# Order of half-height and full-height matrix products in an expert part and a latent stage, and identity products at another wait

## The chip, the cores and the metric

The kernel runs on one core of a Trainium2 chip. The metric is device time in microseconds (us) of one launch, median of several runs; lower is better. A profiled execution supplies the trace.

## The reference, cut to what matters

A small language-model tower on 32 tiles of 128 token rows, 192 features: embedding, an attention, a local-expert attention, then the three parts below.

```python
# latent stage (L), ends with a gated feed-forward network
latent = silu(x_norm @ w_comp);  qkv = latent @ w_qkv            # decayed linear attention ...
x = x + attn_out
xn = rmsnorm(x, ffn_ln_w)
x = x + (silu(xn @ w1) * (xn @ w2)) @ w3                         # 192 -> 512 -> 192
# expert attention (M): 12 heads of 16, softmax, router of 8 experts, top 2
logits = xm @ router_w.T + router_b
# expert part (X)
for e in range(E):
    h = gelu(xm @ w1[e] + b1[e]);  y = h @ w2[e] + b2[e]         # 192 -> 768 -> 192
    out = out + combine[:, e:e + 1] * y
```

## The kernel before

All arithmetic is in float32 in these parts, and each float32 product stands in the trace as two TensorE records (two passes), a transpose as one. Every engine has a program written out by hand; semaphores order them, and `per(g, n, k)` is the value to wait for in turn g.

**Two streams (L and M).** The 32 tiles make 16 pairs. Two streams of pairs, `streams[0]` and `streams[1]`, each own four PSUM banks (`a.bank[0..3]`), and `first(...)` of one pair is interleaved with `second(...)` of the other: the programs are Python generators, `alternate` runs them in turns up to each `yield`, and this fixes the order on every engine. `in_turns_apart(eng, first, second, over, ...)` (L) and `in_turns_routed` (M) are the outer loops: a peeled start, a hardware loop of 7 turns (6 in M) with two pairs each, a peeled end. `over()` is called after the peeled start, at the end of each turn and at the very end.

**Latent stage, hidden layer.** `hidden(a, f, p)` (L1660 to L1669) is called for p = 0 and 1. The 192 input features lie as 128 (`xT[:, 0]`) and 64, the latter doubled into both halves of the partitions (`xT[:, 1]`). For each of `lw_1` and `lw_2` it issues two full-height products (L1665, 128 rows of contraction) and then two half-height ones (L1668, 64 rows, in the two halves of the array, into two banks). ScalarE's silu of it is L1796, VectorE's product L1615. Just behind `hidden` in TensorE's order stand the transposes L1691 of the other pair, which wait for VectorE's L1558. ScalarE's program of the stage uses Identity (L977), Silu (L1743, L1796) and Exp (L1765), and table loads stand in it where the function table changes.

**Expert attention.** `scores(... turned=True)` (L1987) makes the scores of tile 0 and then of tile 1 of the pair; ScalarE exponentiates them (L2116, four per tile). The scores of tile 1 wait for the four exponentials of tile 0, since they use the same banks; between the two stand the router products of the other pair (L2075). `m_times_v` (L2000) of tile 0 waits for the first exponential of tile 1. `stirred(a, n)` (L2015) issues n products of the identity matrix with itself whose result nobody reads; they fill waits. Two stand before the wait for `f.x` (normalised rows, VectorE L1856) at the head of `tensor_m_1`, which the transposes L966 follow.

**Expert part.** The rows that the router sent to each expert are taken in 39 groups of 256 rows, three buffers deep (`h` = 0 to 2), 13 turns of three. For each group SyncE loads the expert's weights (L2267) and rows (L2271) as soon as the group three before it is out (`x_out`); VectorE doubles 64 columns of the rows (L2226); TensorE turns them (L2300, L2301, bank 6); ScalarE takes them out (L2359). TensorE's group is: `up` p = 0 and 1, the turning of the next group's rows, `down` 0, `up` 2, `down` 1, `down` 2. One `up` is two full-height products (L2316) and two half-height ones (L2320), 256 columns each, into banks 0 and 1 (p = 0, 2) or 2 and 3; ScalarE's gelu is L2368. One `down` is four products of 192 columns (L2331) into banks 4 and 5. VectorE weights the result (L2220) and GpSimd adds it to DRAM rows by two indirect transfers (L2249); before the next group's it waits until both have landed (`x_add`).

Of the kernel before, what the change touches and what calls it, by code (L numbers as in the profile page):

```python
# [16 lines left out]
P = 128  # L17
T = 32
D = 192
# [76 lines left out]
def tower(nc, a, out):  # L96

    with ExitStack() as ctx:
# [1245 lines left out]
        def scalar_rest(act):  # L1344
            act.wait_ge(s_loop, 1)
            act.wait_ge(s_wf, 16 * len(loads_f))
            in_turns_apart(act, lambda g, a: scalar_f_1(act, g, a, f_signals(a)),
                           lambda g, a: scalar_f_2(act, g, a, f_signals(a)), at_end=lambda: scalar_l_rates(act))
            scalar_ends(act, F_ENDS, F_SEMS, L_STARTS)
            scalar_l_powers(act)  # L1350
            in_turns_apart(act, lambda g, a: scalar_l_1(act, g, a, l_signals(a)),
                           lambda g, a: scalar_l_2(act, g, a, l_signals(a)))
            act.wait_ge(s_wm, 16 * len(loads_m))
            scalar_ends(act, L_ENDS, L_SEMS, M_STARTS)
            in_turns_routed(act, lambda g, a, prev: scalar_m_1(act, g, a, m_signals(a), prev),
                            lambda g, a, prev: scalar_m_2(act, g, a, m_signals(a), prev),
                            lambda g, a: scalar_routed(act, g, a, m_signals(a)))
            scalar_x(act)
# [301 lines left out]
        def hidden(a, f, p):  # L1660

            for wa, wb, out in ((lw_1a, lw_1b, slice(0, NM)), (lw_2a, lw_2b, slice(NM, 2 * NM))):
                for n in range(2):
                    c = 2 * p + n
                    nc.tensor.matmul(a.bank[c][:, out], wa[:, c * P:(c + 1) * P], a.xT[:, 0, :], start=True, stop=False)  # L1665
                for n in range(2):
                    s = slice(HE * n, HE * (n + 1))
                    mm = nc.tensor.matmul(a.bank[2 * p + n][:, out], wb[s, p * P:(p + 1) * P], a.xT[s, 1, :], start=False,  # L1668
                                          stop=True)  # L1669
            mm.then_inc(f.hid_p, 1)  # L1670
# [34 lines left out]
        def tensor_l_2(pe, g, a, f):  # L1705
# [16 lines left out]
            mm.then_inc(f.ffn_p, 1)  # L1722

# [293 lines left out]
        def tensor_m_1(pe, g, a, f, prev):  # L2017
            stirred(a, 2)
# [30 lines left out]
            yield  # L2049
            pe.wait_ge(f.exp, per(g, 4 * M, 4))  # L2050
            scores(pe, g, a, f, 1, f.scoresT, True)
            stirred(streams[1 - a.n], 2)
# [125 lines left out]
        def vector_x(v, ch):  # L2178
# [28 lines left out]
            def outputs(g, h, first=False):  # L2207
# [11 lines left out]
                for t in range(NT):  # L2219
                    ins = nc.vector.scalar_tensor_tensor(out=x_y[h][:, t, :], in0=bank[4 + t][:, 0:D], scalar=w(t),  # L2220
                                                         in1=x_y[h][:, t, :], op0=ALU.mult, op1=ALU.add)
# [70 lines left out]

        def tensor_x(pe):
# [11 lines left out]
            def up(g, h, p, first=False):  # L2305
                if p == 0:
                    pe.wait_ge(x_xT, per(g, B3, h + 1))
                    pe.wait_ge(x_w[h], per(g, 96, 96))
                    if h > 0 or not first:
                        pe.wait_ge(x_gelu, per(g, B3 * PAIRS, h * PAIRS))  # L2310
                elif p == 2:
                    pe.wait_ge(x_gelu, per(g, B3 * PAIRS, h * PAIRS + 1))
                b = (0, 2, 0)[p]
                for n in range(2):
                    q = p + PAIRS * n
                    nc.tensor.matmul(bank[b + n][:, 0:NR], xw_1a[h][:, q * P:(q + 1) * P], x_T[h][:, 0, :], start=True,  # L2316
                                     stop=False)
                for n in range(2):
                    s = slice(HE * n, HE * (n + 1))
                    mm = nc.tensor.matmul(bank[b + n][:, 0:NR], xw_1b[h][s, p * P:(p + 1) * P], x_T[h][s, 1, :], start=False,  # L2320
                                          stop=True)
                mm.then_inc(x_up, 1)

            def down(g, h, p):
# [3 lines left out]
                for n in range(2):  # L2328
                    f = p + PAIRS * n
                    for t in range(NT):  # L2330
                        mm = nc.tensor.matmul(bank[4 + t][:, 0:D], x_hid[f][:, t * P:(t + 1) * P], xw_2[h][:, f, :],  # L2331
                                              start=(p == 0 and n == 0), stop=(p == PAIRS - 1 and n == 1))
# [3 lines left out]
            def group_of(g, h, more, first=False):  # L2336
                up(g, h, 0, first)
                up(g, h, 1)
                if more:
                    turn_rows(*((g, h + 1) if h < B3 - 1 else (g + 1, 0)))  # L2340
                down(g, h, 0)
                up(g, h, 2)
                down(g, h, 1)
                down(g, h, 2)
# [10 lines left out]
        def scalar_x(act):  # L2355
# [7 lines left out]
            def group_of(g, h, more):  # L2363
                for p in range(PAIRS):
                    act.wait_ge(x_up, per(g, B3 * PAIRS, h * PAIRS + p + 1))
                    for n in range(2):
                        q = p + PAIRS * n
                        ins = nc.scalar.activation(x_hid[q], bank[(0, 2, 0)[p] + n][:, 0:NR], ACT.Gelu,  # L2368
                                                   bias=xb_1[h][:, q:q + 1])
                    ins.then_inc(x_gelu, 1)  # L2370
                    if p == 1 and more:
                        take_rows(*((g, h + 1) if h < B3 - 1 else (g + 1, 0)))
# [142 lines left out]
```

## Time and profile before

| | |
|---|---|
| median of 3 runs | 2048.46 us (2047.97 to 2050.29) |
| profiled execution | 2050.18 us |
| its span in the trace | 2048.5 us |
| mean granted TensorE clock | 0.862 of full speed |
| TensorE busy, matmul | 1606.7 us (78%) |
| VectorE busy | 1309.3 us (64%) |
| ScalarE busy | 976.1 us (48%) |
| GpSimd busy | 400.1 us (20%) |
| latent stage | about 705 to 1200 us of the span |
| expert attention | about 1215 to 1630 us |
| expert part | about 1655 to 2048 us |

The profiled execution took 1.7 us more than the median. A granted clock of 1.00 is 2.4 GHz, 0.50 is 1.2 GHz; a mean between them is a mix of stretches at either level.

### The profile page before, as it was taken

The page shows a single profiled execution, that of the slowest core. Times are in us where ns is not written, and L with a number is a line of the kernel's source. Part 1 is how long each engine was busy: PE and PEld are TensorE (multiplying, and loading weights), DVE is VectorE, ACT ScalarE, POOL GpSimd, SP SyncE. Part 2 cuts the span into 40 slices and gives each one's busy share as a digit, 9 for nine tenths or more (in the row PEclk, how much of TensorE's full clock was granted, in tenths as well). Part 3 has the DMA queues.
Part 4 walks back from the last instruction along what each step waited for, and adds up shares of the span by engine and source line. Part 5 has one row for each costly group of instructions (what it writes and reads, how often), then busy time and mean ns, then how long its engine had stood idle before and what let it go on. Part 6 is the DMA issues. An engine that isn't in the chain of part 4 may idle for free.

```text
span 2048.5 us, 36437 instructions
## 1 busy us (share of the span) xinstructions
PE 1606.7 (78%) x12540; PEld 1167.9 (57%) x12540; DVE 1309.3 (64%) x4361; ACT 976.1 (48%) x2773; POOL 400.1 (20%) x494
## 2 busy tenths in 40 slices
PE   0166673978888668888888868999999769999996
PEld 0032222865665445555555547777877647777774
DVE  7898885878888777887787844666666622222121
ACT  1275998944444444455555423344444324444441
POOL 7302332000000100000000010222222223333332
PEclk9985555557788779999999978999999979999998
DMA  3000001049960000000000000000000057777775
GB/s 73 16 1 1 1 1 17 6 95 185 181 97 0 1 1 1 0 0 0 0 0 0 0 26 1 25 24 23 23 23 27 20 138 178 179 181 175 185 175 128
DMA packets 136262, 113.00 MB, mean 55 GB/s; under 512 B 29416, under 2 KB 128456, under 8 KB 136136
## 3 DMA queue, kind: packets, MB, share of 16 engines
q1 hardware_dynamic: 119320, 91.70, 19.4%
q0 software_dynamic: 16864, 20.33, 5.2%
q8 instruction: 41, 0.67, 0.1%
q14 instruction: 37, 0.30, 0.1%
HBM read 69.19 MB, written 45.94 MB: 56 GB/s over the span
## 4 chain that ended last, share of the span: by engine, by line
PE 51%; DVE 27%; ACT 15%; issue 4%; POOL 1%; DMA 0%; DVEq 0%; ACTq 0%; POOLq 0%; SPq 0%
ACT bank L716 8%; PE bank L2331 8%; PE bank L1007 6%; PE bank L2316 5%; PE bank L2320 4%; PE bank L1987 3%; PE bank L1000 2%; PE bank L1217 2%; PE bank L1665 2%; PE bank L966 2%; DVE R L1839 2%; DVE WK L1581 1%; DVE R L1581 1%; PE bank L2015 1%; PE bank L2000 1%
## 5 line engine op out<-in xcount | busy, mean ns | idle before, releaser
L1047 POOL TENSOR_TENSOR WK<-WK,mhalf 128x2 f32<-128x2 f32 (+1 forms) x96 | 78.0, 813 | 837.4 <-DVE WK L1505 328.3
L2368 ACT ACTIVATE R<-bank,R 128x256 f32<-128x256 f32 x234 | 98.3, 472 | 217.9 <-PE bank L2320 217.9
L2220 DVE SCALAR_TENSOR_TENSOR WK<-bank,R,WK 128x192 f32<-128x192 f32 x78 | 28.9, 412 | 266.6 <-PE bank L2331 266.6
L716 ACT ACTIVATE bank<-bank,nbias,sc 128x128 f32<-128x128 f32 x384 | 168.9, 952 | 21.7 <-POOL nbias L528 21.7
L1007 PE MATMUL bank<-WK,R 96*128 96x256 f32 x576 | 159.1, 421 | 17.0 <-ACT WK L973 11.0
L2249 POOL DMA_INDIRECT moe_sum<-WK x78 | 121.6, 1558 | 258.4 <-DVE WK L2220 197.2
L2331 PE MATMUL bank<-R 128*128 128x192 f32 x936 | 169.1, 331 | 0.0
L716 ACT ACTIVATION_READ_ACCUMULATOR bank<-bank,nbias,sc 128x1 f32 x384 | 162.2, 727 | 0.0
L2331 PEld LDWEIGHTS bank<-R 128*128 128x128 f32 x936 | 150.1, 190 | 13.3 <-issue 13.3
L1007 PEld LDWEIGHTS bank<-WK,R 96*128 96x128 f32 x576 | 111.3, 204 | 41.6 <-ACT WK L973 15.6
L2316 PE MATMUL bank<-R 128*128 128x256 f32 x468 | 126.1, 392 | 1.1 <-ACT R L2359 1.1
L610 PE MATMUL bank<-R 32*128 32x128 bf16 x384 | 62.8, 300 | 60.1 <-ACT bank L716 57.2
L610 PEld LDWEIGHTS bank<-R 32*128 32x128 bf16 x384 | 29.5, 118 | 118.8 <-ACT bank L716 106.7
L2316 PEld LDWEIGHTS bank<-R 128*128 128x128 f32 x468 | 84.5, 192 | 21.1 <-issue 13.2
L1665 PE MATMUL bank<-WK,R 128*128 128x256 f32 x256 | 75.8, 420 | 15.0 <-ACT WK L993 15.0
L433 DVE TENSOR_REDUCE neg_all<-bank 128x3 f32<-128x384 f32 x128 | 69.4, 553 | 27.4 <-PE bank L610 25.2
L966 PE MATMUL bank<-ident,WK 128*96 128x128 f32 x320 | 55.0, 299 | 40.5 <-DVE WK L1030 26.1
L2320 PE MATMUL bank<-R 64*128 64x256 f32 x468 | 83.2, 433 | 0.0
L1987 PE MATMUL bank<-WK 32*128 32x128 f32 x1536 | 64.0, 297 | 24.4 <-ACT R L2116 12.3
L559 PE MATMUL bank<-R,wq 96*128 96x512 bf16 x192 | 78.6, 537 | 4.6 <-DVE WK L407 2.7
L1000 PE MATMUL bank<-R,WK 96*128 96x192 f32 x384 | 76.3, 343 | 2.9 <-ACT WK L973 1.4
L528 POOL TENSOR_SCALAR nbias<-neg_all,sc 128x3 f32<-128x3 f32 x128 | 38.8, 303 | 198.3 <-DVE neg_all L433 198.0
(496 smaller groups left out, 3971.2 us busy)
## 6 DMA issues: line engine op xcount, KB each, us to landing
moe_rows_in<-zeros SPq DMA_DIRECT2D x1, 25026.0 KB, 146.2
R<-in_L_ffn_w SPq DMA_DIRECT2D x39, 576.0 KB, 5.0
R<-in_L_ffn_w SPq DMA_DIRECT2D x39, 384.0 KB, 3.0
R<-moe_rows_in SPq DMA_DIRECT2D x39, 194.0 KB, 4.7
R<-in_L_ffn_w SPq DMA_DIRECT2D x78, 96.0 KB, 3.7
R<-in_L_ffn_b SPq DMA_DIRECT2D x39, 96.0 KB, 5.4
moe_sum<-resid POOLq DMA_DIRECT2D x16, 192.0 KB
moe_sum<-WK POOLq DMA_INDIRECT x78, 5.9
```

The costliest lines, as they stand in the source:

```text
L610: mm = nc.tensor.matmul(bank[u % 4][:, k * P:(k + 1) * P], qk[32 * j:32 * j + 32, k, i * P:(i + 1) * P], qk[32 * j:32 * j + 32, 3 + k, i * ...
L716: ins = nc.scalar.activation(s, s, ACT.Exp, bias=nbias[:, u, k:k + 1], scale=col(SS), accum_out=units(sum_all, g, u)[:, k:k + 1])
L966: mm = nc.tensor.transpose(a.bank[b][0:C, c * NM + i * P:c * NM + (i + 1) * P], src[:, i, c * C:(c + 1) * C], ident[:, :])
L1000: mm = nc.tensor.matmul(a.bank[b][:, i * D:(i + 1) * D], a.xT[0:C, c, i * P:(i + 1) * P], w[0:C, c, :], start=(c == 0), stop=(c == 1))
L1007: mm = nc.tensor.matmul(out, w[0:C, c, m], a.xT[0:C, c, :], start=(c == 0), stop=(c == 1))
L1665: nc.tensor.matmul(a.bank[c][:, out], wa[:, c * P:(c + 1) * P], a.xT[:, 0, :], start=True, stop=False)
L1987: mm = nc.tensor.matmul(a.bank[j][:, k * P:(k + 1) * P], x, y, start=True, stop=True)
L2249: pool.indirect_dma_start(out=acc, out_offset=bass.IndirectOffsetOnAxis(ap=x_id[k % B3][:, t:t + 1].bitcast(U32), axis=0), in_=x_y[k % B3] ...
L2316: nc.tensor.matmul(bank[b + n][:, 0:NR], xw_1a[h][:, q * P:(q + 1) * P], x_T[h][:, 0, :], start=True, stop=False)
L2320: mm = nc.tensor.matmul(bank[b + n][:, 0:NR], xw_1b[h][s, p * P:(p + 1) * P], x_T[h][s, 1, :], start=False, stop=True)
L2331: mm = nc.tensor.matmul(bank[4 + t][:, 0:D], x_hid[f][:, t * P:(t + 1) * P], xw_2[h][:, f, :], start=(p == 0 and n == 0), stop=(p == PAIRS ...
L2368: ins = nc.scalar.activation(x_hid[q], bank[(0, 2, 0)[p] + n][:, 0:NR], ACT.Gelu, bias=xb_1[h][:, q:q + 1])
```

## The change

1. Latent stage: `hidden` issues, for p = 0, all four full-height products and then all four half-height ones; for p = 1 the half-height ones first and then the full-height ones.
2. Latent stage, ScalarE: `over` is now one Silu of 128x1, at the end of the peeled start and of each turn.
3. Expert attention: the two identity products at the head of `tensor_m_1` and the two before the first product with values go; five are put before the wait for the exponentials of tile 0.
4. Expert part: a group is now all six half-height products (`up_rests`, banks 0 to 5), then `up` 0, 1, 2 (full height only), the turning of the next rows, and `down` 0, 1, 2, which go to one bank (7). All gelus of the group before must be done before `up_rests`. ScalarE takes the turned rows after its third gelu pair, not after the second.

```diff
                           lambda g, a: scalar_l_1(act, g, a, l_signals(a)),
-                           lambda g, a: scalar_l_2(act, g, a, l_signals(a)))
+                           lambda g, a: scalar_l_2(act, g, a, l_signals(a)), lambda: scalar_l_silu())
...
+        def scalar_l_silu():
+            nc.scalar.activation(still[:, 1:2], mhalf[:, 0:1], ACT.Silu)
...
         def hidden(a, f, p):
+            first, second = slice(0, NM), slice(NM, 2 * NM)
+            def wholes():
+                for w, out in ((lw_1a, first), (lw_2a, second)):
+                    for c in (2 * p, 2 * p + 1):
+                        mm = nc.tensor.matmul(a.bank[c][:, out], w[:, c * P:(c + 1) * P], a.xT[:, 0, :], ...)
+                return mm
+            def rests():
+                for w, out in ((lw_1b, first), (lw_2b, second)):
+                    for n in range(2):
+                        s = slice(HE * n, HE * (n + 1))
+                        mm = nc.tensor.matmul(a.bank[2 * p + n][:, out], w[s, p * P:(p + 1) * P], a.xT[s, 1, :], ...)
+                return mm
+            if p == 0:
+                wholes()
+                rests().then_inc(f.hid_p, 1)
+            else:
+                rests()
+                wholes().then_inc(f.hid_p, 1)
...
         def tensor_m_1(pe, g, a, f, prev):
-            stirred(a, 2)
             pe.wait_ge(f.x, per(g, 1, 1))
...
             scores(pe, g, a, f, 0, f.scoresT, True)
             yield
+            stirred(streams[1 - a.n], 5)
             pe.wait_ge(f.exp, per(g, 4 * M, 4))
             scores(pe, g, a, f, 1, f.scoresT, True)
-            stirred(streams[1 - a.n], 2)
             pe.wait_ge(f.exp, per(g, 4 * M, 5))
             m_times_v(a, f, 0)
...
+            def up_rests(g, h, first=False):
+                pe.wait_ge(x_xT, per(g, B3, h + 1))
+                pe.wait_ge(x_w[h], per(g, 96, 96))
+                if h > 0 or not first:
+                    pe.wait_ge(x_gelu, per(g, B3 * PAIRS, h * PAIRS))
+                for p in range(PAIRS):
+                    for n in range(2):
+                        s = slice(HE * n, HE * (n + 1))
+                        nc.tensor.matmul(hidden_at(p, n), xw_1b[h][s, p * P:(p + 1) * P], x_T[h][s, 1, :], ...)
+            def up(h, p):
+                for n in range(2):
+                    q = p + PAIRS * n
+                    mm = nc.tensor.matmul(hidden_at(p, n), xw_1a[h][:, q * P:(q + 1) * P], x_T[h][:, 0, :], ...)
                 mm.then_inc(x_up, 1)
...
-                        mm = nc.tensor.matmul(bank[4 + t][:, 0:D], x_hid[f][:, t * P:(t + 1) * P], xw_2[h][:, f, :],
+                        mm = nc.tensor.matmul(bank[7][:, t * D:(t + 1) * D], x_hid[f][:, t * P:(t + 1) * P], xw_2[h][:, f, :],
...
             def group_of(g, h, more, first=False):
-                up(g, h, 0, first)
-                up(g, h, 1)
+                up_rests(g, h, first)
+                for p in range(PAIRS):
+                    up(h, p)
                 if more:
                     turn_rows(*((g, h + 1) if h < B3 - 1 else (g + 1, 0)))
-                down(g, h, 0)
-                up(g, h, 2)
-                down(g, h, 1)
-                down(g, h, 2)
+                for p in range(PAIRS):
+                    down(g, h, p)
...
-                    if p == 1 and more:
-                        take_rows(*((g, h + 1) if h < B3 - 1 else (g + 1, 0)))
+                if more:
+                    take_rows(*((g, h + 1) if h < B3 - 1 else (g + 1, 0)))
```

## Rows read from the trace of the kernel before

**Rows 1.** Timeline of TensorE's matmuls over one group: start, us, line, operation, count.

```profile
1800.30 1.03 PE L2316 MATMUL bank<-R 128*128 128x256 f32 x4
...
1804.60 1.03 PE L2316 MATMUL bank<-R 128*128 128x256 f32 x4
1805.55 0.70 PE L2320 MATMUL bank<-R 64*128 64x256 f32 x4
1806.19 1.13 PE L2316 MATMUL bank<-R 128*128 128x256 f32 x4
1807.25 0.70 PE L2320 MATMUL bank<-R 64*128 64x256 f32 x4
...
1808.37 1.47 PE L2331 MATMUL bank<-R 128*128 128x192 f32 x8
1809.68 1.03 PE L2316 MATMUL bank<-R 128*128 128x256 f32 x4
```

**Rows 2.** Groups of instructions, 1700 to 1950 us: half-height weight loads.

```profile
L2320 PEld LDWEIGHTS bank<-R 64*128 64x128 f32 x320 | 24.1, 184 | 26.5 <-issue 26.5
```

**Rows 3.** Timeline of the other engines, same group and the next.

```profile
1804.80 0.74 DVE L2220 SCALAR_TENSOR_TENSOR WK<-bank,R,WK 128x192 f32<-128x192 f32 x2 [7.47 <-PE bank L2331]
...
1806.30 0.84 ACT L2368 ACTIVATE R<-bank,R 128x256 f32<-128x256 f32 x2 [2.15 <-PE bank L2320]
...
1808.16 1.55 POOL L2249 DMA_INDIRECT moe_sum<-WK  x1 [0.30 <-issue]
...
1815.43 0.23 DVE L2226 COPY R<-R 128x128 f32<-128x128 f32 x1 [0.52 <-DMA R<-moe_rows_in]
...
1815.68 1.55 POOL L2249 DMA_INDIRECT moe_sum<-WK  x1 [5.96 <-DVE WK L2220]
```

**Rows 4.** DMA issues, 1700 to 1950 us: count, median us to landing.

```profile
moe_sum<-WK POOLq DMA_INDIRECT x54, 5.9
```

**Rows 5.** DMA issues, 2012 to 2036 us, where no loads run beside them.

```profile
moe_sum<-WK POOLq DMA_INDIRECT x6, 3.5
```

**Rows 6.** Groups of ScalarE, 720 to 1200 us: two of its table loads.

```profile
L977 ACT ACT_TABLE_LOAD x7 | 9.0, 1283 | 0.1
L1743 ACT ACT_TABLE_LOAD x7 | 9.0, 1283 | 0.1
```

**Rows 7.** Timeline around such loads.

```profile
931.02 1.13 PE L1007 MATMUL bank<-WK,R 96*128 96x256 f32 x4 [0.57 <-ACT WK L977]
932.28 0.38 ACT L1743 ACTIVATE R<-bank 128x256 f32<-128x256 f32 x1
```

**Rows 8.** Timeline behind the hidden layer of the latent stage.

```profile
914.41 1.03 DVE L1558 SCALAR_TENSOR_TENSOR WK<-WK 128x384 f32<-128x384 f32 x2
...
915.17 1.53 PE L1691 MATMUL bank<-ident,WK 128*128 128x128 f32 x12
...
917.44 0.95 PE L1639 MATMUL bank<-R 32*128 32x128 f32 x24 [0.74 <-ACT R L1769]
...
918.53 1.01 DVE L1581 TENSOR_TENSOR WK<-bank,decay 128x384 f32<-128x384 f32 x2
```

**Rows 9.** Timeline of TensorE in the expert attention (PEld is the weight load).

```profile
1473.90 0.95 PE L1987 MATMUL bank<-WK 32*128 32x128 f32 x24 [0.71 <-ACT R L2116]
...
1475.46 0.86 PE L2000 MATMUL bank<-R 128*32 128x128 f32 x24
...
1476.93 0.39 PEld L966 LDWEIGHTS bank<-ident,WK 128*96 128x96 f32 x4 [0.15 <-DVE WK L1856]
```

**Rows 10.** Busy time by stretch: stretch, length, PE, PEld, DVE, ACT, POOL, granted clock, DMA.

```profile
1255.14:1601.71 346.57, 321.73 (x3498) 273.51 (x3497) 227.09 (x891) 142.24 (x337) 88.05 (x106) 0.96 0.07 23
1448.69:1452.10 3.41, 3.31 (x40) 2.83 (x44) 1.49 (x9) 1.63 (x5) 1.01 (x1) 0.50 0.00 0
1356.11:1404.54 48.43, 44.53 (x503) 37.83 (x501) 33.00 (x131) 20.22 (x49) 13.26 (x16) 1.00 0.07 25
1404.54:1454.83 50.29, 47.09 (x502) 40.21 (x501) 33.00 (x131) 20.43 (x49) 13.26 (x16) 0.93 0.07 24
```

More of the change, by code:

```diff
@@ L1660, in hidden @@
         def hidden(a, f, p):
[L1662 to L1670, printed above, removed]
+            first, second = slice(0, NM), slice(NM, 2 * NM)
+            def wholes():
+                for w, out in ((lw_1a, first), (lw_2a, second)):
+                    for c in (2 * p, 2 * p + 1):
+                        mm = nc.tensor.matmul(a.bank[c][:, out], w[:, c * P:(c + 1) * P], a.xT[:, 0, :], start=(p == 0 and w is lw_1a),
+                                              stop=(p == 1), skip_group_check=True)
+                return mm
[3 more added lines that the diff above has]
+                        s = slice(HE * n, HE * (n + 1))
+                        mm = nc.tensor.matmul(a.bank[2 * p + n][:, out], w[s, p * P:(p + 1) * P], a.xT[s, 1, :],
+                                              start=(p == 1 and w is lw_1b), stop=(p == 0), skip_group_check=True)
+                return mm
[5 more added lines that the diff above has]
+                wholes().then_inc(f.hid_p, 1)
         def tensor_l_1(pe, g, a, f):
@@ L2219, in outputs @@
                 for t in range(NT):
-                    ins = nc.vector.scalar_tensor_tensor(out=x_y[h][:, t, :], in0=bank[4 + t][:, 0:D], scalar=w(t),
+                    ins = nc.vector.scalar_tensor_tensor(out=x_y[h][:, t, :], in0=bank[7][:, t * D:(t + 1) * D], scalar=w(t),
                                                          in1=x_y[h][:, t, :], op0=ALU.mult, op1=ALU.add)
@@ L2291, in sync_x, with hidden_at @@
             sp.wait_ge(x_end_st, 16)
+        def hidden_at(p, n):
+            return bank[2 * p + n][:, 0:NR]
         def tensor_x(pe):
@@ L2303, in turn_rows @@
                 mm.then_inc(x_turned, 1)
[L2305 to L2313, printed above, removed]
+            def up_rests(g, h, first=False):
[6 more added lines that the diff above has]
+                        s = slice(HE * n, HE * (n + 1))
+                        nc.tensor.matmul(hidden_at(p, n), xw_1b[h][s, p * P:(p + 1) * P], x_T[h][s, 1, :], start=True, stop=False)
+            def up(h, p):
                 for n in range(2):
                     q = p + PAIRS * n
[L2316 to L2321, printed above, removed]
+                    mm = nc.tensor.matmul(hidden_at(p, n), xw_1a[h][:, q * P:(q + 1) * P], x_T[h][:, 0, :], start=False, stop=True)
                 mm.then_inc(x_up, 1)
@@ L2330, in down @@
                     for t in range(NT):
-                        mm = nc.tensor.matmul(bank[4 + t][:, 0:D], x_hid[f][:, t * P:(t + 1) * P], xw_2[h][:, f, :],
-                                              start=(p == 0 and n == 0), stop=(p == PAIRS - 1 and n == 1))
+                        mm = nc.tensor.matmul(bank[7][:, t * D:(t + 1) * D], x_hid[f][:, t * P:(t + 1) * P], xw_2[h][:, f, :],
+                                              start=(p == 0 and n == 0 and t == 0), stop=(p == PAIRS - 1 and n == 1),
+                                              skip_group_check=True)
                 if p == PAIRS - 1:
@@ L2367, in group_of @@
                         q = p + PAIRS * n
-                        ins = nc.scalar.activation(x_hid[q], bank[(0, 2, 0)[p] + n][:, 0:NR], ACT.Gelu,
-                                                   bias=xb_1[h][:, q:q + 1])
+                        ins = nc.scalar.activation(x_hid[q], hidden_at(p, n), ACT.Gelu, bias=xb_1[h][:, q:q + 1])
                     ins.then_inc(x_gelu, 1)
-                    if p == 1 and more:
-                        take_rows(*((g, h + 1) if h < B3 - 1 else (g + 1, 0)))
+                if more:
+                    take_rows(*((g, h + 1) if h < B3 - 1 else (g + 1, 0)))
             take_rows(0, 0)
```

## The prediction

> **What bounds the kernel now.** I read the page's clock and busy rows first, then the chain of waits stage by stage, then timelines. Three stages are touched, and each has another limit.
>
> In the expert part TensorE sets the pace. The group that has its second `up` at 1800.30 is followed by the same step at 1809.68: a period of 9.38 us [rows 1], and there are 39 groups. No matmul of these rows carries a wait of its own; its time is products plus something at each change between full and half height. The other engines wait for it: VectorE 7.47 us, ScalarE 2.15 us, GpSimd 5.96 us [rows 3].
>
> In the latent stage the chain of waits goes back and forth between ScalarE, VectorE and TensorE, so only what lies on it counts. On it, once per turn, stand ScalarE's table loads before L977 and L1743 [rows 6, 7].
>
> In the expert attention the clock drops. Two turns of two pairs each, the same work: 48.43 us at clock 1.00, 50.29 us at a mean of 0.93 [rows 10]. One 3.41 us stretch at half clock (the 1.2 GHz level) begins at 1448.69, behind router products that stream 8 columns and a wait for exponentials such as the idle 0.71 us [rows 9]. The reader is to see that this wait costs little by itself, and that a half-clock stretch follows it.
>
> **Expert part, step by step.** From the starts [rows 1]: four full-height records that come from full-height work last 0.95 until the half-height ones; four that come from half-height work last 1.06; so entering costs 0.11. Four half-height records, two at a time, last 0.64 including an entry and an exit: 1.06 less 0.64 is two full passes, 0.21 each, and 0.95 less four of them leaves about 0.1 for the exit. Eight records of 192 columns take 1.31, or 0.164 each, which is 0.218 for 256 columns: the same pass, 0.215. A change of height thus costs 0.20 in all. Before, a group changes height six times (three `up`s, in and out). After, twice. Nothing else is added on TensorE: 18 pass times (12 full, 6 pairs of halves) at 0.215, 24 at 0.164, four turns at 0.11 and two changes give 3.87 + 3.94 + 0.43 + 0.40 = 8.64; the same sum with six changes gives 9.44 against the measured 9.38. Saving: 4 x 0.20 = 0.80 a group, 39 x 0.80 = 31 us. New period 8.58.
>
> What must stay hidden. Count from the start of the half-height run: it ends at 1.5, the `up`s end at about 2.4, 3.2 and 4.1, the turning at 4.6, the `down`s at 5.9, 7.2, 8.6. Two gelus take 0.84 [rows 3], so they end at about 3.5, 4.4 and 5.2; `down` needs them at 4.6, 5.9 and 7.2. The smallest slack is 1.1 us. The new wait of `up_rests` for all gelus needs 5.2 against 8.6. Row take-out ends near 6.3, needed at 8.6; a table load of about 1.3 behind it is covered as well. One output bank in place of two: VectorE is done 0.9 us into the next group, `down` writes at 4.6. The next rows: output done at 1805.54, doubled copy at 1815.43 to 1815.66 [rows 3], 10.1 us later. TensorE turns them now 11.7 us after the output (its period of 9.38, plus 3.3 to the turning, less 0.9) and after the change 8.6 + 4.2 - 0.8 = 12.0. Turning later in the group pays for the shorter period. That is why I price the transfers at nothing; if they grew by 2 us, the excess would be paid in every group.
>
> The tight one is GpSimd. It issues its second indirect transfer at 1808.16, 0.30 + 1.55 after the first (so 1806.31), waits for it to land, and needs about 0.7 to restart (the first came 0.77 after the output was done, 1804.80 + 0.74): with the median landing of 5.9 [rows 4] a cycle of 8.5; the period before is an upper bound, since at 1815.68 VectorE released it, not the transfer [rows 3]. So its cycle is 8.5 to 9.3, against 8.58 needed. But without loads beside it a landing takes 3.5 [rows 5], so a late transfer meets the idle tail of each load burst and gets faster, and it has three buffers to be late in. I take no loss; the bound is 0.4 us a group.
>
> The price of a long half-height run isn't in the trace, which has only runs of two pairs. Nearest rows: a pass pair of 0.215 (two loads of 0.184 overlap) up to 0.32, if each pair paid the entry. The four loads are recorded 184 ns each [rows 2] while the whole block of four lasts 0.64, so they overlap. I take 0.215.
>
> The Trainium skill speaks against this: "TensorE: Matmul & The Clock Gate", Part 3, says that a weight load overlaps matmuls in flight only where the row group differs, so that in a long run of half-height products, every second load would have to wait for its own half. No row of before settles it for half height.
>
> **Latent stage.** Hidden layer: eight changes of height per pair become two (one in the middle, since p = 0 ends and p = 1 begins with halves, one back, and the transposes follow full-height work), so the block is 6 x 0.20 = 1.2 us shorter. But the transposes L1691 behind it start at 915.17, and they need the first half of L1558 (914.41 + 0.52 = 914.93): only 0.24 can be won. Further on, VectorE's L1581 could start at the end of L1639, 918.39, and starts at 918.53 [rows 8], so of it 0.14 to 0.24 comes through. 15 pairs x 0.15 = 2.3, and the last pair, alone, gets its whole 1.2.
>
> Silu: the table state at the loop's head is now the same from both sides, so I expect the seven loads at L977 and the seven at L1743 to go [rows 6]. The added Silu of one column, under the 0.38 of L1743's 256, lies where TensorE is still busy with L1000. TensorE was idle 0.57 before L1007 for L977 and L1743 started 0.13 after L1007's end (931.02 + 1.13); without loads both go, and the matmuls' modelled tail (1.13 less an entry and four passes, 0.16) overlaps: 0.70 to 0.86 a turn [rows 7]. Seven turns x 0.86 = 6. Together 9 us, bounds 5 and 12.
>
> **Expert attention.** Five identity products are ten records of 128 columns, half a pass each: 1.08 us, and about 0.2 to change to the scores' shape. They fill the 0.71 of waiting and 0.16 of the tail before it, so the scores of tile 1 (L1987, 1473.90) come 0.4 later. Behind them the exponentials and L2000 shift alike, from 1475.46 to 1475.86; the two products that stood there are gone. L2000 then ends near 1476.7, and L966 waits for VectorE's L1856 until 1476.93 in any case [rows 9]. The delay ends there, with 0.2 us to spare; without that cover it would cost 16 x 0.4 = 6 us. The removed products at the head won nothing either, for the same reason. What counts is the clock: between 1255.14 and 1601.71 lie 14 pairs in 346.57 us, mean clock 0.96 [rows 10]. A turn of two pairs without a half-clock stretch takes 48.43, so seven take 339.0. So half-clock stretches cost 7.5 us here. Five products in the poorest place should remove nearly all: 7 us, bounds +6 (they stay and the delay surfaces) and -9 (one more at the stage's start goes too).
>
> **Sum.** 31 + 9 + 7 = 47 us off the profiled 2050.2 gives 2003; the median lies 1.7 lower than that execution: 2001.5.
>
> **The rivals.**
> GpSimd's transfers become the bound of the expert part: a cycle of 9.0 saves 0.38 a group, 15 us in place of 31: 2017. For it: the 8.5 to 9.3 above. Against: the lateness heals itself.
> The smaller edits do nothing: table loads stay (they are placed by the program's builder, not by the kernel's text) and the clock drops stay: 2001.5 + 6 + 7 = 2014.5. Against: the expert attention's loop has none, though Exp is used there.
> Each half-height pair pays 0.32: 6 x 0.105 = 0.63 of the 0.80 is eaten, 0.17 x 39 = 7 us are left, the hidden layer's 3.5 are lost: 2029.
> Slower: weight loads and passes of one half don't overlap. A pair then takes load and matmul, 0.184 + 0.215 = 0.40, up to 0.43 with what a change drains. At 0.43 the six pairs add 1.29 and save 0.80: +0.49 x 39 = 19; the hidden layer +4; tables and clock -13: 2050.2 + 10 - 1.7 = 2058. It decides from 0.35 in the expert part alone, and from about 0.41 over the kernel. For it: the cited rule. Against: full-height loads overlap the pass before, and the first pair in a run is issued together.
>
> **How the numbers follow.** Forecast 0.69, GpSimd 0.12, small edits 0.10, half-height 0.32 0.05, slower 0.04. The likeliest spans 1993 (33, 13, 9 saved) to 2011. The range adds GpSimd's and the small edits' cases: 1993 to 2019, leaving out about 0.12. Within 0.2% is 4 us, about what a measurement of this kernel can tell from no change. Faster 0.94; same 0.02, where the pair takes about 0.40; slower 0.04.
>
> **What would show it.** The period of L2316 blocks 8.6; one run of twelve L2320 records in about 1.5 us; GpSimd released by its own transfer in many groups, with a landing near 6. No table loads at L977 and L1743 in the loop; L1691 released by L1558. L966 still released by L1856, mean clock near 1.00 in the attention's loop. Wrong would be: a run of halves of over 2 us; ScalarE or a row transfer as releaser of TensorE in the expert part; clock drops in new places.

## The result and the profile after

The changed kernel takes 2002.2 us (median of four runs, 2001.13 to 2004.31); the kernel before took 2048.45 beside it (2047.97 to 2050.29). The ratio is 0.9774 [0.9757, 0.9791]: 46 us less. The forecast was 2001.5, its range 1993 to 2019.

The profiled execution has a span of 2000.0 us, against 2048.5 before. Cut at ScalarE's first latent row, at the attention's first exponential, at the first doubled copy of rows and at the last output, the 48.5 us of difference in span lie as follows:

| stretch | before | after | difference | forecast |
|---|---|---|---|---|
| up to the first latent row of the latent stage (no line of it changed) | 720.4 | 718.3 | -2.1 | 0 |
| latent stage | 525.5 | 520.0 | -5.6 | -9 |
| expert attention | 412.6 | 401.9 | -10.7 | -7 |
| expert part, to its last output | 371.6 | 341.8 | -29.8 | -31 |
| what follows | 18.4 | 18.1 | -0.3 | 0 |

The sum was right to a microsecond; the terms were not. Two errors cancelled: the latent stage took 3.4 us more than forecast, the attention 3.7 less.

**Expert part.** TensorE's timeline of one group (start, busy time, line, shapes, count, in brackets the idle time before it and what ended it). It answers to [rows 1]; L2334 are the half-height products, L2339 the full-height ones, L2349 `down`:

```profile
1796.38 4.07 PE L2349 MATMUL bank<-R 128*128 128x192 f32 x24
1800.38 1.57 PE L2334 MATMUL bank<-R 64*128 64x256 f32 x12
1801.87 2.86 PE L2339 MATMUL bank<-R 128*128 128x256 f32 x12
1804.57 0.27 PE L2321 MATMUL bank<-ident,R 128*128 128x128 f32 x1
...
1805.00 4.07 PE L2349 MATMUL bank<-R 128*128 128x192 f32 x24
1809.00 1.57 PE L2334 MATMUL bank<-R 64*128 64x256 f32 x12
```

From 1800.38 to 1809.00 is a period of 8.62 us; the forecast was 8.58. Twelve half-height records last 1.49 from their start to that of the next block. The runs of four in [rows 1] last 0.64, two passes and 0.21 of changing; with the same 0.2 in it, the run of twelve has 1.29 for six pairs, 0.215 each: two halves still share one pass.

GpSimd's waits between 1700 and 1950 us (waiting engine and line, released by; us in total, times, longest), first after:

```profile
POOL moe_sum L2266 <- DMA moe_sum<-WK: 140.1, 27, 6.1
POOL moe_sum L2266 <- DVE WK L2237: 15.6, 3, 5.2
```

then the kernel before:

```profile
POOL moe_sum L2249 <- DVE WK L2220: 124.2, 21, 6.1
POOL moe_sum L2249 <- DMA moe_sum<-WK: 29.8, 5, 6.0
```

The releaser has changed sides, as forecast: in 27 of 30 waits it is now GpSimd's own transfer. TensorE doesn't notice: between 1700 and 1950 us it has no wait in the trace, before or after.

**Latent stage.** The table loads between 720 and 1200 us (count; us in total and mean ns; idle before):

```profile
L1783 ACT ACT_TABLE_LOAD x16 | 20.5, 1283 | 0.3
L1814 ACT ACT_TABLE_LOAD x15 | 19.2, 1283 | 0.3
L1740 ACT ACT_TABLE_LOAD x1 | 1.3, 1283 | 0.0
```

The fourteen of [rows 6] are gone; one at the new Silu, ahead of the loop, has come. The block of the hidden layer, which answers to [rows 8]:

```profile
909.83 1.99 PE L1667 MATMUL bank<-WK,R 128*128 128x256 f32 x8 [0.94 <-ACT WK L993]
911.76 2.00 PE L1675 MATMUL bank<-WK,R 64*128 64x256 f32 x16
913.69 1.99 PE L1667 MATMUL bank<-WK,R 128*128 128x256 f32 x8
915.86 1.03 DVE L1558 SCALAR_TENSOR_TENSOR WK<-WK 128x384 f32<-128x384 f32 x2
916.47 1.53 PE L1705 MATMUL bank<-ident,WK 128*128 128x128 f32 x12 [0.79 <-DVE WK L1558]
```

The three runs last 5.7 us, where the block before lasts 6.8 (from 908.39 to the start of L1691 at 915.17). The transposes behind them, L1705, now wait for VectorE's L1558, as the forecast said.

What it did not foresee stands in the windows (start and end; length, then busy us and count of TensorE, its weight loads, VectorE, ScalarE, GpSimd; granted clock, DMA share, GB/s). Two stretches of one turn each, two pairs, and a piece of the first:

```profile
820.00:877.23 57.23, 47.59 (x390) 35.22 (x387) 44.16 (x135) 27.51 (x77) 4.92 (x6) 0.90 0.00 0
942.02:999.25 57.23, 45.83 (x404) 32.89 (x402) 47.40 (x148) 28.27 (x79) 4.92 (x6) 1.00 0.00 0
808.24:818.48 10.24, 9.76 (x23) 6.40 (x21) 4.51 (x13) 4.14 (x13) 1.31 (x2) 0.50 0.00 0
```

A turn of two pairs at clock 1.00 has a length of 57.23 us. In the first stretch the same length doesn't hold a whole turn (135 VectorE instructions, not 148), because the clock was at half speed for part of it. Inside the loop of the kernel before there were two stretches at half clock of 3.4 us each. Now there are five, 30.7 us in all: of 3.4 us at 787.8, 849.2 and 1139.3, and of 10.2 us at 808.2 and 869.7.

**Expert attention.** A window inside the loop (cut otherwise than the earlier one, so the two lengths aren't to be compared), and one pair, which answer to [rows 10] and [rows 9]:

```profile
1250.30:1580.00 329.70, 302.03 (x3464) 258.53 (x3462) 224.86 (x884) 137.51 (x328) 87.97 (x106) 1.00 0.07 24
```

```profile
1455.23 1.36 PE L2033 MATMUL bank<-ident 128*128 128x128 f32 x10
1456.52 0.95 PE L2005 MATMUL bank<-WK 32*128 32x128 f32 x24
1458.08 0.86 PE L2018 MATMUL bank<-R 128*32 128x128 f32 x24 [0.61 <-ACT R L2133]
1459.12 0.64 PE L966 MATMUL bank<-ident,WK 128*96 128x128 f32 x4 [0.17 <-DVE WK L1874]
```

The clock stays at 1.00 from 1224.7 to 1607.0 us, so through the whole loop. The later scores cost nothing: a turn of two pairs takes 48.45 us, where a clean one took 48.43 before, and L966 still waits for VectorE, now 0.17 us. The cover that is left is 0.17 where the forecast had 0.2.

### The profile page after: what moved, and what is told of

Same layout as the page of the kernel before. It is cut to its first block, busy times and chain, and to the rows that moved or that the text cites. A ratio compares the mean times of both kernels' runs of the same rounds, so it can differ in the third digit from the quotient of the medians.

```text
span 2000.0 us, 36491 instructions
## 1 busy us (share of the span) xinstructions
PE 1549.0 (77%) x12572; PEld 1182.7 (59%) x12572; DVE 1314.1 (66%) x4361; ACT 959.7 (48%) x2769; POOL 399.4 (20%) x494
## 4 chain that ended last, share of the span: by engine, by line
PE 50%; DVE 31%; ACT 12%; issue 4%; POOL 2%; DVEq 0%; DMA 0%; ACTq 0%; POOLq 0%; SPq 0%
ACT bank L716 8%; PE bank L2349 8%; PE bank L1007 6%; PE bank L2339 5%; PE bank L2334 3%; PE bank L1000 3%; PE bank L1217 2%; PE bank L2005 2%; PE bank L966 2%; DVE R L1581 2%; DVE R L1857 2%; DVE WK L1581 2%; PE bank L1667 1%; PE bank L1705 1%; PE bank L640 1%
## 5 line engine op out<-in xcount | busy, mean ns | idle before, releaser
L1007 PE MATMUL bank<-WK,R 96*128 96x256 f32 x576 | 159.2, 421 | 13.7 <-ACT WK L973 11.0
L2349 PE MATMUL bank<-R 128*128 128x192 f32 x936 | 158.6, 326 | 0.0
L2349 PEld LDWEIGHTS bank<-R 128*128 128x128 f32 x936 | 151.3, 190 | 0.1
L2339 PE MATMUL bank<-R 128*128 128x256 f32 x468 | 112.6, 391 | 0.0
L2339 PEld LDWEIGHTS bank<-R 128*128 128x128 f32 x468 | 86.6, 192 | 23.6 <-issue 13.2
L610 PEld LDWEIGHTS bank<-R 32*128 32x128 bf16 x384 | 29.5, 118 | 118.8 <-ACT bank L716 106.6
L966 PE MATMUL bank<-ident,WK 128*96 128x128 f32 x320 | 54.3, 295 | 46.8 <-DVE WK L1030 27.7
L433 DVE TENSOR_REDUCE neg_all<-bank 128x3 f32<-128x384 f32 x128 | 69.5, 554 | 27.3 <-PE bank L610 25.2
L1667 PE MATMUL bank<-WK,R 128*128 128x256 f32 x256 | 69.8, 420 | 15.0 <-ACT WK L993 15.0
L1000 PE MATMUL bank<-R,WK 96*128 96x192 f32 x384 | 77.7, 347 | 2.8 <-ACT WK L973 1.4
L2115 ACT ACTIVATE WK<-bank,R 128x256 f32<-128x256 f32 x96 | 40.3, 470 | 69.7 <-PE bank L1007 69.7
```

The costliest lines, as they stand in the source:

```text
L610: mm = nc.tensor.matmul(bank[u % 4][:, k * P:(k + 1) * P], qk[32 * j:32 * j + 32, k, i * P:(i + 1) * P], qk[32 * j:32 * j + 32, 3 + k, i * ...
L966: mm = nc.tensor.transpose(a.bank[b][0:C, c * NM + i * P:c * NM + (i + 1) * P], src[:, i, c * C:(c + 1) * C], ident[:, :])
L1000: mm = nc.tensor.matmul(a.bank[b][:, i * D:(i + 1) * D], a.xT[0:C, c, i * P:(i + 1) * P], w[0:C, c, :], start=(c == 0), stop=(c == 1))
L1007: mm = nc.tensor.matmul(out, w[0:C, c, m], a.xT[0:C, c, :], start=(c == 0), stop=(c == 1))
L1667: mm = nc.tensor.matmul(a.bank[c][:, out], w[:, c * P:(c + 1) * P], a.xT[:, 0, :], start=(p == 0 and w is lw_1a), stop=(p == 1), skip_grou ...
L2339: mm = nc.tensor.matmul(hidden_at(p, n), xw_1a[h][:, q * P:(q + 1) * P], x_T[h][:, 0, :], start=False, stop=True)
```

## The experiments

Each ratio is to the kernel before, timed on the same chip. The groups ran on different chips; the median of the kernel before lies between 2047.9 and 2049.3 in all of them, so times are also subtracted directly, from group to group to about 1 us. Stage lengths are those of one profiled execution each, cut as above, and that execution can lie some us off the median: 5.9 above it for ident_none, 4.2 for ident_only.

### First group: each part alone

Here the kernel before took 2047.91 us.

**x_only** takes the new order of the expert part and leaves all else as before:

```
+                up_rests(g, h, first)
+                for p in range(PAIRS):
+                    up(h, p)
...
+                for p in range(PAIRS):
+                    down(g, h, p)
```

> The kernel before with only the expert part changed. My theory (a change between full and half height costs 0.20 us, four fewer per group, 39 groups): period of a group 8.6 us, 30 to 31 us less than before, ratio 0.985. Rival, the transfers of GpSimd as bound: about 15 us less.

It took 2018.31, ratio 0.9851 [0.9836, 0.9866]. The period is 8.62 and the part lasts 342.2 us against 371.6: 29.4 less in the profile, 29.6 in the time of the kernel. The part stands alone, and needs nothing from the others.

**hidden_only** takes `wholes` and `rests` in the hidden layer alone:

```
+            if p == 0:
+                wholes()
+                rests().then_inc(f.hid_p, 1)
+            else:
+                rests()
+                wholes().then_inc(f.hid_p, 1)
```

> The kernel before with only the order of the latent stage's hidden layer changed. My theory: the block is 1.2 us shorter, but the work behind it is released by VectorE, so a turn of two pairs without half-clock stretches goes from 58.43 to about 58.1 and the kernel wins 2 to 3 us; extra half-clock stretches behind the shortened block can take that back (0 to 4 us slower). Rival, the block is on the path: 16 x 1.2 = 19 us less.

2041.06, ratio 0.9967 [0.9955, 0.9979]: 6.8 less, over twice what was expected. But by stage, the latent stage is 1.9 us shorter, the expert attention 4.8 and the untouched part before both 2.2. The attention has no changed line in this kernel; it had 6 stretches of half clock before its last one, where the kernel before has 8. So a kernel's time carries away the luck of its clock, and a part's worth can't be read from it to a few microseconds.

**silu_only** takes the one added Silu ahead of the loop:

```
+                           lambda g, a: scalar_l_2(act, g, a, l_signals(a)), lambda: scalar_l_silu())
...
+            nc.scalar.activation(still[:, 1:2], mhalf[:, 0:1], ACT.Silu)
```

> The kernel before with only the added Silu. My theory: the fourteen table loads at L977 and L1743 go, 0.86 us less in each of seven turns, 6 us in all. Rival, the loads were covered: nothing, or 0.2 us a turn slower.

2040.43, ratio 0.996 [0.9947, 0.9974]: 7.5 less, of which 5.4 in the latent stage, 0.9 in the attention and 1.1 ahead of both.

**ident_only** moves the identity products:

```
-            stirred(a, 2)
...
+            stirred(streams[1 - a.n], 5)
             pe.wait_ge(f.exp, per(g, 4 * M, 4))
             scores(pe, g, a, f, 1, f.scoresT, True)
-            stirred(streams[1 - a.n], 2)
```

> The kernel before with only the identity products of the expert attention moved. My theory: half-clock stretches of this stage's loop go, 7 us, and some 3 us at its start; 10 us less. Rival, the five products only delay the scores by 0.4 us a pair: 0 to 6 us slower, with clock drops as before.

2034.21, ratio 0.9935 [0.9921, 0.9948]: 13.7 less. The attention is 11.0 us shorter, with clock 1.00 from 1250 to 1610 us. The forecast's bound of 9 for this part was passed. It allowed for one stretch at the stage's start beside those of the loop; the first step there, from one pair's exponentials to the next pair's, gains 3.3 by itself. The 2.7 by which the time gained more than the stage aren't placed.

The four parts add up to 57.6 us, the whole change gives 46. Most of the missing 11 lies in two stages. In the attention the profiled executions of the four add up to 16.7 us, the whole gives 10.7: hidden layer and Silu each shifted its drops in their favour, 4.8 and 0.9, and with the products moved no drops are left in the loop to shift. In the latent stage they add up to 7.4, the whole gives 5.6: the two alone had 79.7 and 62.7 us at half clock, together 79.7, where the kernel before has 59.2. The other 3 are differences of 0.6 to 1.1 in the other three stretches.

### Second group: the rivals of the expert part, and the clock

Here the kernel before took 2049.27.

**x_mixed** is the changed kernel with the expert part's banks and waits, but `up`'s halves put back behind each pair's full-height products, so that a group changes height six times:

```
-                    mm = nc.tensor.matmul(hidden_at(p, n), xw_1a[h][:, q * P:(q + 1) * P], x_T[h][:, 0, :], start=False, stop=True)
+                    nc.tensor.matmul(hidden_at(p, n), xw_1a[h][:, q * P:(q + 1) * P], x_T[h][:, 0, :], start=True, stop=False)
+                for n in range(2):
+                    s = slice(HE * n, HE * (n + 1))
+                    mm = nc.tensor.matmul(hidden_at(p, n), xw_1b[h][s, p * P:(p + 1) * P], x_T[h][s, 1, :], start=False, stop=True)
```

> The changed kernel, but in the expert part each of the three steps has its two full-height products and then its two half-height ones, as before; banks, waits and the order of steps are those of the change. Six changes of height a group in place of two. My theory: a group takes 9.4 us again, the kernel 30 us more than the changed one, about 2032. Rival, the order of the steps and the later taking of rows made the gain: about 2002.

2027.47, ratio 0.9896 [0.988, 0.9911]:

```profile
1800.50 1.03 PE L2335 MATMUL bank<-R 128*128 128x256 f32 x4
1801.46 0.70 PE L2338 MATMUL bank<-R 64*128 64x256 f32 x4
1802.09 1.13 PE L2335 MATMUL bank<-R 128*128 128x256 f32 x4
...
1809.88 1.03 PE L2335 MATMUL bank<-R 128*128 128x256 f32 x4
```

The period is 9.38 again, and the part lasts 371.2 us, 29.5 more than after. The order of `up` and `down`, the banks and the later take-out of rows are the new ones here; they bring nothing. All of the gain is the four changes of height, 0.76 us a group or 0.19 each. (The kernel as a whole loses only 25, since its latent stage, whose code is the same, met a kinder clock: 69.5 us at half speed against 79.7, and 3.4 us shorter.)

**x_short** leaves the third pair of `down` products out, to ask how much more TensorE could give before GpSimd's transfers set the pace (the second pair then waits for all three gelus):

```
-                for p in range(PAIRS):
+                for p in range(PAIRS - 1):
                     down(g, h, p)
```

> The changed kernel without the third pair of down products of each group (a third of the second product is left out, so the output is another), which takes 1.3 us off TensorE's group: 7.3 us if nothing else binds. My theory: GpSimd's own cycle (two transfers, landing, restart) is just under 8.6, so the group will take 8.2 to 8.6 and the kernel wins at most 15 us against the changed one. Rival, GpSimd's cycle shrinks with its lateness: 7.5 or less, 45 us less.

It took 1950.69, in a single run: 51.5 less than the changed kernel, of which the expert part has 49.6. The period is 7.32:

```profile
1805.38 1.57 PE L2334 MATMUL bank<-R 64*128 64x256 f32 x12
1808.10 1.55 POOL L2266 DMA_INDIRECT moe_sum<-WK  x1 [3.79 <-DMA moe_sum<-WK]
1812.70 1.57 PE L2334 MATMUL bank<-R 64*128 64x256 f32 x12
```

My theory, a floor of 8.2 to 8.6 set by the transfers, falls. From 1700 to 1900 us GpSimd's waits for its own transfer are more, but shorter; the changed kernel first, then x_short:

```profile
POOL moe_sum L2266 <- DMA moe_sum<-WK: 109.2, 21, 6.1
POOL moe_sum L2266 <- DMA moe_sum<-WK: 110.1, 28, 4.7
```

The median landing is 5.6 us, 5.9 in the changed kernel. In the same window the first transfer of a group starts 1.6 to 4.0 us after its output is done, 0.8 to 2.0 in the changed kernel, and the lateness falls again after each rise. So the cycle is elastic: there is at least another 1.3 us a group to be had from TensorE before it counts.

**ident_none** is the changed kernel without its five identity products at the wait for the exponentials. The two pairs that the change took away are gone here as well. Eleven others stay, as in both kernels: 5, 5 and 1 per pair ahead of the waits for VectorE's row maxima (`f.rowmax`), which `stirred` also fills:

```
-            stirred(streams[1 - a.n], 5)
```

> The changed kernel without the five identity products at the wait for the exponentials, and without those that the change took away, too. My theory: half-clock stretches come back in the expert attention, 8 to 15 us more than the changed kernel. Rival, the gain came from taking the others away: the same time or 3 us less.

2020.43, ratio 0.9859 [0.9844, 0.9874]: 18 more than the changed kernel, over the upper end of what was expected. Its attention, first, and that of ident_only, whose code there is the changed kernel's:

```profile
1250.00:1610.00 360.00, 323.31 (x3399) 269.43 (x3398) 229.90 (x908) 145.36 (x338) 87.94 (x106) 0.90 0.07 22
```

```profile
1250.00:1610.00 360.00, 331.15 (x3756) 283.72 (x3756) 240.88 (x946) 150.89 (x359) 93.55 (x113) 1.00 0.07 24
```

Without the five there is a stretch of half clock in every pair, 3.4 or 6.8 us long, 112.6 us in the stage, and its pairs take 24.9 and 26.3 us in turn against 23.85 and 24.60. With two products at each of two places (before) it was 63.1, with five at one place 33.2, of which nothing lies in the loop. The profiled execution shows the stage 21.2 us longer; by the medians these five are worth 18 us. So taking the others away made no gain. Whether it is the place or one product more that makes five better than two and two was not tried.

**l_fill** uses the same means in the latent stage, whose loop had got the new drops: three identity products ahead of the wait for the attention's output, three ahead of the wait for the turned rows of the hidden layer:

```
+            filled(a, 1, 3)
             pe.wait_ge(f.out, per(g, M, M))
...
             turn_doubled(a, a.xr, 2, f.xT_p)
+            filled(a, 3, 3)
             pe.wait_ge(f.xT, per(g, 3, 3))
```

> The changed kernel with three identity products at two waits of the latent stage (before the attention's output is turned, and before the hidden layer), where TensorE is idle 0.9 to 1.3 us. My theory: the half-clock stretches of this stage's loop, which cost the changed kernel about 7 us, go: 1995 to 1997. Rival, the products delay what follows and the clock drops elsewhere: 2002 or more.

1991.86, ratio 0.9721 [0.9708, 0.9734]: faster than the changed kernel by 10. TensorE after, then in l_fill:

```profile
804.81 1.20 PE L1657 MATMUL bank<-ident,R 128*128 128x128 f32 x6
807.38 0.64 PE L966 MATMUL bank<-ident,R 128*96 128x128 f32 x4 [1.36 <-DVE R L1592]
807.96 0.86 PE L966 MATMUL bank<-ident,WK 128*96 128x128 f32 x4
808.70 2.93 PE L1000 MATMUL bank<-R,WK 96*128 96x192 f32 x8
```

```profile
804.85 1.20 PE L1657 MATMUL bank<-ident,R 128*128 128x128 f32 x6
805.89 0.83 PE L1689 MATMUL bank<-ident 128*128 128x128 f32 x6
807.41 0.64 PE L966 MATMUL bank<-ident,R 128*96 128x128 f32 x4 [0.69 <-DVE R L1592]
807.99 0.64 PE L966 MATMUL bank<-ident,WK 128*96 128x128 f32 x4
808.74 1.57 PE L1000 MATMUL bank<-R,WK 96*128 96x192 f32 x8
```

L966 starts 2.57 and 2.56 us after L1657: the products lie wholly inside the wait. Then L1000 takes 2.93 at half clock and 1.57 without. That is the effect at this place. The latent stage lasts 510.1 us, 9.9 less than after, with no half clock between 747.5 and 1184.4 us, so none in its loop behind the first turn.

### Third group: what the small edits are worth when the clock is still

l_fill has no drops in either loop, so it is a steadier ground on which to undo an edit. Here the kernel before took 2048.69.

**fill_old_hidden** is l_fill with the hidden layer of the kernel before:

```
+            for wa, wb, out in ((lw_1a, lw_1b, slice(0, NM)), (lw_2a, lw_2b, slice(NM, 2 * NM))):
+                for n in range(2):
+                    ...
```

> The kernel with identity products at two waits of the latent stage, but with the hidden layer's order of before. With the clock held up, this shows what the new order is worth by itself. My theory (the block's 1.2 us are mostly covered by VectorE's work): turns of two pairs are 0.34 us longer, the last pair 1.2, so 3 to 4 us more than with the new order. Rival, the block is on the path: 19 us more.

1996.57, ratio 0.9746 [0.9732, 0.9759]: 4.7 more than l_fill. The latent stage is 5.3 longer. From one latent silu (L1743 before) to the next its steps are 28.54 and 28.95 us in turn, where l_fill has 28.35 and 28.85: 0.29 a turn, 2 us in all. The other 3.4 come behind the last of these turns, where the half clock is 3.4 us longer too.

**fill_no_silu** is l_fill without the added Silu:

```
-                           lambda g, a: scalar_l_2(act, g, a, l_signals(a)), lambda: scalar_l_silu())
+                           lambda g, a: scalar_l_2(act, g, a, l_signals(a)))
```

> The same filled kernel without the added Silu. My theory: the fourteen table loads are back, 0.86 us a turn, 6 us more than with it, all in seven longer turns. Rival, what the Silu run won over before was partly clock luck: 3 us or less.

2000.4, ratio 0.9762 [0.9749, 0.9775]: 8.5 more. The latent stage is 6.5 longer; every second of these steps is 29.78 against 28.85, 0.93 a turn. Six such steps and another 0.97 behind the last of them are the 6.5. The other 2 aren't placed: the profiled executions differ by 6.9 only.

**fill_one** keeps only the second of l_fill's two places:

```
-            filled(a, 1, 3)
             pe.wait_ge(f.out, per(g, M, M))
```

> The filled kernel with identity products only before the hidden layer, not before the attention's output is turned. My theory: there are two weak places per pair for the clock, one filled; some half-clock stretches stay, 2 to 5 us more than with both. Rival, the place before the hidden layer is the one that counts: the same as with both, about 1992.

1996.47, ratio 0.9743 [0.973, 0.9757]: 4.6 more than l_fill, 6 less than the changed kernel. Three stretches of 3.4 us at half clock are left, where the changed kernel has three of 3.4 and two of 10.2. Each of the two places does part.

**f_fill** is l_fill with identity products in the local-expert attention too, four ahead of the wait for `x` and three ahead of that for the turned rows:

```
+            for _ in range(4):
+                nc.tensor.matmul(a.bank[1][:, 0:P], ident[:, :], ident[:, :], start=True, stop=True)
             pe.wait_ge(f.x, per(g, 1, 1))
             turn(a, a.x, 0, f.xTp)
+            for _ in range(3):
+                nc.tensor.matmul(a.bank[1][:, 0:P], ident[:, :], ident[:, :], start=True, stop=True)
             pe.wait_ge(f.xT, per(g, 1, 1))
```

> The filled kernel with seven more identity products per pair in the local-expert attention (four before the normalised rows are turned, three before the turned rows are read), where TensorE is idle 0.7 to 1.6 us and the clock is at the lower level for some 110 us. My theory: fewer half-clock stretches there too, 3 to 12 us less than without: 1980 to 1989. Rival, ScalarE and VectorE bound that stage, or the products delay it: 1990 or more.

1970.17, ratio 0.9616 [0.9603, 0.9629]: 21.7 less than l_fill, nearly twice the upper end of what was expected. Windows over this attention, l_fill first:

```profile
500.00:718.00 218.00, 172.01 (x984) 124.72 (x983) 174.95 (x735) 96.09 (x352) 13.75 (x21) 0.80 0.41 71
```

```profile
500.00:697.00 197.00, 160.95 (x1120) 118.31 (x1116) 168.71 (x726) 94.24 (x345) 13.75 (x21) 0.95 0.45 79
```

and the same products in l_fill and in f_fill:

```profile
604.07 2.06 PE L1007 MATMUL bank<-WK,R 96*128 96x256 f32 x4 [0.68 <-ACT WK L973]
605.92 1.70 PE L1217 MATMUL bank<-R,WK 96*128 96x224 f32 x4
```

```profile
603.69 0.83 PE L1216 MATMUL bank<-ident 128*128 128x128 f32 x6
604.53 1.13 PE L1007 MATMUL bank<-WK,R 96*128 96x256 f32 x4
605.50 0.92 PE L1221 MATMUL bank<-R,WK 96*128 96x224 f32 x4
```

Four records of 256 columns take 1.13 instead of 2.06 (2.4 and 1.2 GHz). The time at half clock in this stage, from 440 us on, falls from 118.3 to 25.3 us. f_fill beats both kernels: 78.5 us under the one before, some 32 under the changed one.

## Why the prediction was right

**Height changes, 31 us.** Right, 29.8 measured, 29.4 with that part alone, 29.5 lost when the changes come back. A change costs 0.19, not 0.20: the period was 0.04 above the forecast's 8.58, which is 1.6 us over 39 groups.

**Price of a long half-height run, 0.215 a pair.** Right: twelve records in 1.49 us. At 0.32 they would have lasted 2.1, at 0.43 2.8. The Trainium skill's rule that spoke against it ("TensorE: Matmul & The Clock Gate", Part 3: a weight load overlaps matmuls in flight only where the row group differs) isn't borne out here: no load surfaces in the run of halves, nor in the full-height blocks, where all loads have the same rows and twelve records take 2.70 us, 0.225 each. The measurement decides.

**What stays hidden.** Right. No block of TensorE between 1700 and 1950 us has a wait. GpSimd's own transfer took over as its releaser (27 of 30), and the group isn't longer for it. The forecast's own cycle for GpSimd, 8.5 to 9.3, and the rival's 9.0 were too long: x_short runs at 7.32.

**Latent stage, 9 us: this term was mis-sized, 5.6 measured.** Both of its mechanisms held, near their price. Silu: forecast 0.70 to 0.86 a turn and 6 in all; measured 0.93 a turn and 6.5 by the trace. Hidden layer: forecast 0.15 a pair and 2.3 + 1.2; measured 0.29 a turn, the same 0.15 a pair, but 3.4 and not 1.2 behind the last turn, 5.3 by the trace and 4.7 in time. What failed is a step that the forecast left out of this stage's term, the clock, though it named drops in new places as a sign of being wrong. The loop had 6.8 us at half clock and got 30.7. Measured from silu to silu of one stream, the six turns that follow the first save 7.2 us when clean (6 x 1.20, from 58.43 to 57.23). But two of them exceed the clean length before, by 3.4 us in all (60.25 and 60.02), and two after, by 8.0 (61.24 and 61.18). So 4.6 of the 7.2 went back, and 2.6 are left; nearly all the rest of the 5.6 comes behind these turns. l_fill shows it by taking the drops away: 9.9 us off the stage, 7.8 of them in the same six turns.

How much the clock gives back isn't fixed by the code. x_mixed, x_short and ident_none are the changed kernel letter for letter up to the end of this stage. Theirs lasts 516.6, 516.1 and 523.5 us, with 69.5, 69.5 and 89.9 us at half clock; the changed kernel's 520.0 has 79.7. Against the 525.5 before, the same edit is thus worth 2.0 to 9.4 us, with one execution read of each kernel. The forecast's 9 lies inside, and the 5.6 is one draw.

**Expert attention, 7 us: mis-sized, 10.7 measured.** The mechanism held: clock 1.00 in the loop, no delay surfacing, L966 released by VectorE. The forecast set the gain at 7.5 from 14 pairs [rows 10] and rounded down; its bound was 9. Counted from one pair's exponentials to the next pair's, the first step went from 25.99 to 22.72, 3.3 less, and the 14 that follow from 347.1 to 338.4, 8.7 less; behind them 1.3 went back. So what was mis-sized is mostly the start, where the forecast put nothing and allowed for one stretch at most.

**Nothing ahead of the latent stage: 2.1 measured.** Code and work are the same there. The half clock in the local-expert attention (from 440 us on) was 125.1 us before and 111.4 after. x_only and ident_only, which have the same code up to the end of the latent stage as before, show 125.1 both; x_mixed and x_short, two kernels with equal code there, show 108.0 and 125.1. So it differs between kernels whose code is equal there, and the 2.1 can't be put down to an edit.

**The chance.** That the forecast came within 1 us is luck: measured less forecast is +3.4 in the latent stage, -3.7 in the attention, +1.2 in the expert part and -2.1 ahead of them.

## What to carry to other kernels

Count how often TensorE changes between tile heights, before anything else about its order: here each change costs 0.19 us, 0.38 for going to half height and back, and nothing else about reordering the blocks of the expert part mattered. Read the granted clock over every stage, and where a loop has stretches at half clock, fill its waits of about 1 us with products that nobody reads, at a place where the next instruction waits anyway; six records inside a wait of 1.36 us cost nothing and made L1000 behind them 1.36 us shorter. Price a small edit in a kernel whose clock is still: in one whose clock moves, a stage whose code stays the same gave or took 5 us when something else was edited, and up to 7 between kernels that are equal up to its end.

## What the runs showed of the hardware that I had not expected

- The local-expert attention gave 21.7 us for seven identity products a pair, more than any edit but the expert part's. It had run at half clock for 118 of the 279 us between 440 and 719. A wait of 1.09 us was the longest of the pair that was read, and 1.6 us the longest between 470 and 690 us. The Trainium skill ("TensorE: Matmul & The Clock Gate", "A second HAM failure mode: psum-queue depth-cycling") knows clocks that go up and down where the engine idles briefly between groups of matmuls; that agrees with the rows shown, and that spare products inside those idles stop it is what the runs add.
- Where the drops fall can repeat between kernels (the latent stage's turns in x_mixed and x_short agree to 0.03 us) and can move between kernels that are equal up to there (a turn of 61.18 us in the changed kernel is one of 57.80 in x_mixed). What decides which of several like waits is followed by one stays open.
- The landing of the output transfers didn't grow when the period shrank by 1.3 us: the median is 5.6 us in x_short against 5.9, though the same bytes are moved in less time. Why is open.
